# A gated product moved from VectorE to GpSimd in a chunked delta-rule scan

## What is computed

```
def step(S, inp):
    q_t, k_t, v_t, g_t, b_t = inp
    S = S * jnp.exp(g_t)[..., None, None]
    u = (v_t - jnp.einsum('bhk,bhkv->bhv', k_t, S)) * b_t[..., None]
    S = S + jnp.einsum('bhk,bhv->bhkv', k_t, u)
    o_t = jnp.einsum('bhk,bhkv->bhv', q_t, S)
    return (S, o_t)
...
o = o * lax.rsqrt(jnp.mean(o * o, axis=-1, keepdims=True) + EPS) * norm_w
o = o * jax.nn.silu(gv)
return o.reshape(Bx, Tx, H * DV) @ Wo
```

## Time and profile before

| what | us |
|---|---|
| median of 3 runs | 2638.2 |
| lowest and highest of them | 2637.47, 2646.84 |
| span of the profiled execution | 2632.2 |
| median less that span | 6.0 |
| share of the span: TensorE, VectorE, ScalarE, GpSimd | 86%, 72%, 51%, 43% |

### The profile page before, as it was taken

The page is one execution under the profiler, slowest core; times in us unless marked ns, Lnnn a source line. Parts: engine busy times, 40 slices in busy tenths (PEclk is TensorE's granted clock), DMA queues, the critical chain, the costliest instruction groups (busy, mean ns, idle before and its releaser), DMA issues. The chain is left out here.

```text
span 2632.2 us, 93819 instructions
## 1 busy us (share of the span) xinstructions
PE 2266.7 (86%) x36541; PEld 1651.1 (63%) x36542; DVE 1903.0 (72%) x3913; ACT 1354.1 (51%) x3667; POOL 1137.5 (43%) x1143
## 2 busy tenths in 40 slices
PE   4652999999987889899888989989898888989987
PEld 4541999999963646556565655746556565655646
DVE  5664232323228888988889899888988989888894
ACT  0001444344326655656656566655656656566663
POOL 3774444444433426253342624436253342624333
PEclk9997999999988999999999999999999999999998
DMA  5574222222210010100101000010100101000010
GB/s 168 193 248 152 72 72 73 71 72 72 72 55 21 17 44 11 36 22 25 32 15 44 21 27 23 25 44 5 42 22 25 33 14 44 23 24 22 25 29 16
DMA packets 105644, 135.05 MB, mean 51 GB/s; under 512 B 39360, under 2 KB 78816, under 8 KB 105056
## 3 DMA queue, kind: packets, MB, share of 16 engines
q0 software_dynamic: 23552, 61.38, 7.5%
q1 hardware_dynamic: 62448, 40.55, 5.8%
q10 hardware_dynamic: 19312, 28.33, 3.0%
HBM read 76.18 MB, written 54.00 MB: 49 GB/s over the span
## 5 line engine op out<-in xcount | busy, mean ns | idle before, releaser
L1458 DVE SCALAR_TENSOR_TENSOR att_cv<-att_psA,att_cw,att_cv 128x508 f32<-128x508 f32 (+2 forms) x660 | 479.2, 737 | 7.6
L1789 POOL TENSOR_TENSOR att_Sd<-att_S,att_mst 128x1024 f32<-128x1024 f32 x128 | 242.9, 1903 | 505.1 <-DVE att_S L1572 482.0
L999 PE MATMUL att_psA<-att_xt,att_wqkv 128*128 128x512 f32 x880 | 425.3, 616 | 17.0 <-DMA att_xt<-xn_cols 12.6
L1122 PE MATMUL att_psS<-att_W,att_ktok 128*128 128x128 f32 x2048 | 258.8, 280 | 12.1 <-DVE att_S L1572 6.4
L999 PEld LDWEIGHTS att_psA<-att_xt,att_wqkv 128*128 128x128 f32 x880 | 156.7, 193 | 178.7 <-issue 159.5
L734 PE MATMUL moe_psHT<-moe_xT,moe_w1s 128*128 128x128 f32 x2176 | 267.5, 276 | 0.0
L1122 PEld LDWEIGHTS att_psS<-att_W,att_ktok 128*128 128x128 f32 x2048 | 242.5, 193 | 32.9 <-issue 17.2
L675 ACT ACTIVATE moe_hT<-moe_psHT,moe_b1T 128x128 f32<-128x128 f32 x544 | 155.1, 368 | 201.1 <-PE moe_psHT L734 201.1
L744 PE MATMUL moe_psY<-moe_w,moe_hT 128*128 x1088 | 257.2, 379 | 0.0
L734 PEld LDWEIGHTS moe_psHT<-moe_xT,moe_w1s 128*128 128x128 f32 x2176 | 256.1, 193 | 0.2
L701 DVE TENSOR_TENSOR moe_y<-moe_psY,moe_b2b 128x256 f32<-128x256 f32 x136 | 57.8, 425 | 271.1 <-PE moe_psY L744 271.1
(11 more groups left out here) (247 smaller groups left out, 4382.1 us busy)
## 6 DMA issues: line engine op xcount, KB each, us to landing
expert_out<-moe_y POOLq DMA_DIRECT2D x136, 128.0 KB, 2.0
route_x_in<-in_L_attn_x_dram SPq DMA_DIRECT2D x64, 128.0 KB
xn_rows<-route_xn ACTq DMA_DIRECT2D x16, 512.0 KB, 3.6
xn_cols<-route_xnT ACTq DMA_DIRECT2D x16, 512.0 KB, 3.8
moe_w<-in_L_ffn_W_dram ACTq DMA_DIRECT2D x2, 4096.0 KB, 24.5
att_xt<-xn_cols SPq DMA_DIRECT2D x16, 512.0 KB, 4.4
att_xr<-in_L_attn_x_dram SPq DMA_DIRECT2D x64, 128.0 KB, 2.7
out_dram<-att_xr SPq DMA_DIRECT2D x256, 32.0 KB, 1.7
```

The source lines that it names most:

```text
L999: last = MM(pair_bank(m, j)[:, h, :], wqkv[:, c, (2 * j + h) * P:(2 * j + h + 1) * P], xt[:, c, :], start=(c == 0), stop=(c == DC - 1))
L1122: last = MM(pS[:, h // 4, 2 * DV * (h % 4):2 * DV * (h % 4) + 2 * DV], ktok[:, c % 2, h, :], W[:, h, 2 * two:2 * two + 2, :], start=True, ...
L1458: last = V.scalar_tensor_tensor(out=late, in0=by_lane(pair_bank(m, j)[:, h, :])[:, :, 0:LT - d], scalar=cw[:, 2 * j + h, TAPS - 1 - d:TAPS ...
L1789: G.tensor_tensor(new, old, bc(mst[:, par, c, 4 + 2 * two:6 + 2 * two, :], 3, DV), op=ALU.mult).then_inc(s["sd_done" if two else "sd_half" ...
```

## The change

GpSimd gets one new product per chunk, of O and the gate, in place. It stands after the decayed second half of S and ahead of `factor`; it waits for the squares (its own engine's) and for the gate. VectorE's `scale_out` loses one of its two products: the one that is left multiplies the gated O by the factor and writes O3. The semaphore o2_done goes, og_done comes, and `factor` waits for o3_done of the chunk before, where it waited for o2_done. The sum of squares is still taken of the ungated O.

```diff
             def scale_out(m, c):
                 n = GROUP * m + c
                 wait(dve, "f_done", n + 1)
-                V.tensor_tensor(heads(O[:, :]), heads(O[:, :]), bc(fo[:, :], 2, DV), op=ALU.mult).then_inc(s["o2_done"], 1)
-                wait(dve, "o2_done", n + 1)
-                wait(dve, "gate_done", n + 1)
+                wait(dve, "og_done", n + 1)
                 wait(dve, "otr_ready", n)
-                V.tensor_tensor(O3[:, :], O[:, :], gate[:, c, :], op=ALU.mult).then_inc(s["o3_done"], 1)
+                V.tensor_tensor(heads(O3[:, :]), heads(O[:, :]), bc(fo[:, :], 2, DV), op=ALU.mult).then_inc(s["o3_done"], 1)
...
+            def gated(m, c):
+                n = GROUP * m + c
+                wait(G, "osq_done", n + 1)
+                wait(G, "gate_done", n + 1)
+                G.tensor_tensor(O[:, :], O[:, :], gate[:, c, :], op=ALU.mult).then_inc(s["og_done"], 1)
+
             def factor(m, c):
...
-                wait(G, "o2_done", n)
+                wait(G, "o3_done", n)
                 G.tensor_tensor(fo[:, :], f1[:, :], mhalf[:, :], op=ALU.pow).then_inc(s["f_done"], 1)
...
                     if c < 3:
                         read(m, par, c + 1, 1)
+                    gated(m, c)
                     factor(m, c)
```

More of the change, by code:

```diff
@@ L803, in attention @@
             "vector": "tap taps_done norm_read nq_done nk_done kk_used qk_used elim "
-                      "ks_scaled r_done o_sum s_half s_done ss_done o2_done o3_done acc1_done acc2_done fin_done",
+                      "ks_scaled r_done o_sum s_half s_done ss_done o3_done acc1_done acc2_done fin_done",
             "gpsimd": "wt_done sidx_done k_halo_step k_halo vq_halo_step vq_halo qg_ready knorm_done "
-                      "sd_half sd_done osq_done f_step f_done",
+                      "sd_half sd_done osq_done og_done f_step f_done",
         }
```

## The result

The changed kernel is slower: median 2684.8 us of 4 runs (2681.0 to 2687.8) against 2640.7 us of 4 runs (2637.5 to 2646.8) of the kernel before, a ratio of 1.0161 with a 95% interval of 1.0136 to 1.0185. Its profiled execution took 2681.0 us with a span of 2679.1 us. The forecast was 2661 us in a range of 2640 to 2675: slower was right, the size was not.

What follows compares the result with a forecast made beforehand. The scan was taken as bound by the ring through L1564 and solve, mostly TensorE's work. Late solves cost 23.3 us in full groups and 1.7 in the last, less 1.2 and 0.7 gained: 2661 us, range 2640 to 2675.

Steps and rivals of the forecast that it cites:

- The ring: The scan's recurrent chain: L1564, solve, spread, state update, S, read of the keys, L1564; one chunk takes 13.35 us.
- Who holds whom: GpSimd's new product holds VectorE's L1564, ending it 0.84 us later; solve 0.63 us late twice per group, 0.29 once.
- the near tie: GpSimd's L1803 starts at 1576.48, VectorE's L1564 at 1576.49; the new product takes L1803's place and was expected to win.
- the upper bound's 0.20 us: Part of the forecast's upper bound of 2670 us, which with some 5 us of spread set the range's end.
- the price: Length assumed for GpSimd's new 512-column product, taken from the squares L1796: 1.04 us.
- 23.3: Forecast loss in us over the scan chunks of the 15 full groups, from the late solves.
- The last group: The three scan chunks after the 15 full groups; loss sized at +1.7 us.
- rival 3: TensorE's clock drops in the new gaps, 0.84 us a time; 45 drops add 38 us, 2699 us; chance 7%.
- The fourth chunk's scale_out: Saved VectorE product ahead of L1510: hidden in most groups, 0.6 us gained in each of two, -1.2 us.
- The end: The last product of all, for which TensorE's L1145 waits at 2623.49: -0.7 us.
- Rivals 1 and 2: 1: VectorE wins the tie, 2641 us, 15%; 2: VectorE is the bound, 46 us gained, 2592 us, 6%.

## Why the prediction was right and where it was wrong

- **The bound.** Right. The ring over L1564, solve, spread, L1122 and L1572 set the chunk, and the removed product lay beside it: with VectorE's second product kept and GpSimd's added the loss is the same (1.0156), and with L1564 freed of the hold it is gone (0.9999).
- **Who holds whom.** Right in each part: GpSimd wins the near tie in the full groups (by 4 ns at the least, in 90 places of three profiles), L1564 ends 0.55 us after it, solve starts 0.10 us after R, and nothing takes it back. L1807 goes behind the waiting L1564, so the upper bound's 0.20 us didn't come. The page "SBUF — State Buffer" of the Trainium skill, section "Who interferes with whom", says the same of two SBUF inputs, of a GpSimd instruction that only writes, and of issue order; the runs with PSUM, memset and the other place agree (0.69, 0.69 and 0.74 us). That the hold lasts the whole GpSimd instruction, as the prediction has it from that page, the products bear out and the power doesn't: in the kernel before, 79 VectorE instructions with two SBUF inputs (L1564, L1589, L1594) start inside L1806, at least 0.1 us before its end, and none is longer than without it (0.69, 0.48 and 0.49 us).
- **The step that failed** is the price "L1796 has the same shape, engine and two SBUF inputs: 1.04 us". It has two inputs but one tile: it reads O twice. The product of O and the gate reads two and takes 1.27. The kernel before has no GpSimd product of two full tiles of this width, so the price was an estimate and needed an upper case. The 0.23 us more stand in 45 places on the ring, 45 x 0.23 = 10.4 us, and 23.3 + 10.4 is the 33.7 measured; that it meets to the tenth is luck, since the mean of three profiles is 32.5. The run with one tile read twice puts back 1.04 us, and with it the prediction's chunks, to 0.01 or 0.02 us. The prediction's other estimate, from the Trainium skill's page "GPSIMD Engine Reference", section "Key points", with its factor of about two, gave 1.38 us and 2677 us. It would have been nearer: the measured factor is 1.27 / 0.69 = 1.84.
- **What the price doesn't explain.** With 10.4 us added the forecast is 2671.7 us, still inside its range. The measured span is 23.8 us above the forecast one (2679.1, 2655.3): 10.4 are the price, 1.9 the last group, 0.2 lie before the scans, the end gives 1.5 back, and 12.9 lie between the scans (+11.7, where the forecast had -1.2). The forecast had no term for these stretches but the -1.2, and no allowance for their spread; what lengthened them in the first pair of profiles stays open but for the part that goes with the clock.
- **The last group** was sized at +1.7 and cost +3.6 to it. Its two late solves follow an idle of 2.69 us, where 1.63 stood. The two waits of 1.06 more are 2.1 us, the price again; the other 1.5 us go with TensorE's clock, since more instructions behind them run slowly:

```profile
2642.56 1.93 PE L1105 MATMUL att_psC<-att_R,att_Y 32*32 32x64 f32 x64 [2.69 <-issue]
...
2645.46 1.94 PE L1093 MATMUL att_psC<-att_S,att_qT 128*32 128x64 f32 x64
2647.33 2.62 PE L1122 MATMUL att_psS<-att_W,att_ktok 128*128 128x128 f32 x16
```

  In a full group L1093 takes 1.10 and L1122 2.05. By the granted clock, TensorE is at 1.2 GHz for 10.2 us of the last group in each of the three profiles of the changed kernel, for 6.8 in each of the kernel before. Solve itself was as slow there before (1.93). So of rival 3 there is something in this group, though not at its price, and nothing in the other 45 places, where solve takes 1.10 behind gaps of up to 0.79 and the granted clock stays at 1.00.
- **The fourth chunk's scale_out** was to bring 1.2 us in two groups. The factor came 0.3 us late there, and about 0.4 us a group was left. The wait of L1510 for TensorE grew from 25.4 to 31.2 us: what VectorE was spared was waited out. In the two groups without that wait the pair L1510 begins 0.4 us earlier after the second half of S, 0.8 us in all for the 1.2 forecast.
- **The end** gained 2.2 us, not 0.7. In the kernel before the last row of TensorE, behind the L1145 of the earlier trace rows, is the first below; the changed kernel's last two follow:

```profile
2624.83 3.46 PE L1157 MATMUL att_psS<-att_wo,att_oT 128*128 128x256 f32 x8 [0.69 <-ACT att_oT L1362]
```

```profile
2671.92 0.66 PE L1145 MATMUL att_psS<-ident,att_O 128*128 128x128 f32 x4 [1.19 <-DVE att_O L1607]
2673.26 1.99 PE L1157 MATMUL att_psS<-att_wo,att_oT 128*128 128x256 f32 x8 [0.69 <-ACT att_oT L1362]
```

  L1145's wait for VectorE is 1.19 us for 1.92, the 0.7 of the forecast; the rest is L1157, at 1.99 us for 3.46, which the forecast had no part in: the clock is at 1.2 GHz for 3.6 us of the end before and for none after. With the product behind the factor VectorE is spared the same work, and that L1157 takes 3.05 us, so the gain isn't the spared product's.
- **Rivals 1 and 2** didn't come: the product started ahead of L1564, by 0.02 us in the rows shown, and was never held by it (1282 ns at the most), and no chunk was shorter.
- **The range** was drawn round the length of one instruction taken from a row that only looked like it, with a lower case and no upper one for that length. Its upper end, 2675, lacked both the 10 us of the product and the spread of the stretches between the scans.

## What to carry to other kernels

Before work is moved to GpSimd, look at what VectorE does in the same moment: here an instruction with both inputs in SBUF was held until GpSimd's product of SBUF tiles ended, whatever the engines' busy shares said. If the held one is on the path, place the GpSimd instruction where VectorE's work has slack (here behind the factor, 2.2 us later) or take one of the VectorE inputs from PSUM; either gave all of the loss back, to within 0.2%. And price an instruction from a row with the same operands, not only the same shape; where there is no such row, give the price an upper case.

## What was not expected of the hardware

- A GpSimd product of 128x512 took 1.04 us where it read one tile twice or two inputs with repeated columns (L1776), 1.27 where it read two full tiles, and 0.73 for two tiles of 256 columns.
- When VectorE and two GpSimd instructions in a row compete, VectorE's goes in between them: L1807 took 0.65 us behind L1564 and 0.20 where L1564 read from PSUM.
- Not every GpSimd instruction holds VectorE for its length: the power of 8 columns, 1.67 us long, left an L1564 that began 0.05 us into it at its 0.69 us.
- The unchanged kernel's stretches between the scans varied by 23 us over three profiles on two chips, with the chunks constant to 2 us. Part of that goes with the time at the lower granted clock; the rest was not settled.
